# Cross attention in a four-layer perceiver: one sum over heads for four batches, the last key's share as a fifth slot, and the output product one round later

## The reference

```python
qh, kh, vh = heads(norm(x) @ wq.T + bq), heads(ctx @ wk.T + bk), heads(ctx @ wv.T + bv)
scores = einsum('bhqd,bhkd->bhqk', qh, kh) / sqrt(8) + mask * -1e9
av = einsum('bhqk,bhkd->bhqd', softmax(scores), vh)     # 257 keys
x = x + av.reshape(B, 32, 128) @ wo.T + bo
```

## Time and profile before

| | |
|---|---|
| time, median of 3 runs | 3692.14 us (3683.45 to 3694.7) |
| profiled execution | 3689.13 us, of which the span 3687.2 us |
| PE busy | 2674.5 us (73%) |
| DVE busy | 2416.8 us (66%) |
| ACT busy | 1807.5 us (49%) |
| POOL busy | 1662.8 us (45%) |
| rounds of the three stages touched | 827.9 to 1300.5, 1699.5 to 2173.7, 2770.2 to 3240.4 us of the span (first projection to last addition) |

### The profile page before, as it was taken

One profiled execution on the slowest core, in us unless ns is written; L12 is line 12 of the kernel. 1 busy time (PEld: TensorE's weight loads), 2 busy tenths in 40 slices (PEclk: granted clock), 3 DMA queues, 4 the chain that ended last, 5 costly groups with the idle time before them and its releaser, 6 DMA issues. The chain is left out here.

```text
span 3687.2 us, 98216 instructions
## 1 busy us (share of the span) xinstructions
PE 2674.5 (73%) x27184; PEld 2116.8 (57%) x27185; DVE 2416.8 (66%) x8780; ACT 1807.5 (49%) x5569; POOL 1662.8 (45%) x1768
## 2 busy tenths in 40 slices
PE   5962577739999979757999970367748999978562
PEld 3741466626777669645777740256636777747552
DVE  5965711148999947646999976551148999969615
ACT  2451033328888723325888865213327777734221
POOL 2620055517777700004777740015526777736162
PEclk9975588969999979878999985559979999979665
DMA  2003043421111100201333300214434544400122
GB/s 79 1 0 96 25 118 111 117 75 40 37 37 36 28 7 0 109 0 52 72 74 72 74 25 0 55 42 116 112 87 113 110 111 111 101 1 1 35 88 69
DMA packets 209738, 224.95 MB, mean 61 GB/s; under 512 B 29651, under 2 KB 177619, under 8 KB 208948
## 3 DMA queue, kind: packets, MB, share of 16 engines
q1 hardware_dynamic: 196948, 197.56, 20.5%
q0 software_dynamic: 12672, 25.98, 2.8%
HBM read 201.68 MB, written 21.76 MB: 61 GB/s over the span
## 5 line engine op out<-in xcount | busy, mean ns | idle before, releaser
L1765 ACT ACTIVATE sx<-sx,nm 128x257 f32<-128x257 f32 x1536 | 770.5, 505 | 264.2 <-DVE nm L1809 264.2
L1680 POOL TENSOR_TENSOR sx<-sx,rs 128x1028 f32<-128x1028 f32 x384 | 731.9, 1906 | 372.0 <-DVE rs L1815 372.0
L1809 DVE CUSTOM_DVE_ANT_0 sx<-bank,rows 128x257 f32<-128x257 f32 x1024 | 393.1, 422 | 53.7 <-PE bank L1755 35.5
L247 POOL TENSOR_TENSOR rstd<-var,nhalf 128x16 f32<-128x16 f32 x24 | 69.7, 2905 | 775.3 <-DVE var L264 775.3
L1443 ACT ACTIVATE hT<-bank,B 128x128 f32<-128x128 f32 x714 | 206.0, 368 | 432.2 <-PE bank L1411 260.8
L1469 DVE TENSOR_TENSOR yb<-bank,b2s 128x128 f32<-128x128 f32 x159 | 46.4, 292 | 429.6 <-remote 230.5
L1765 ACT ACTIVATION_READ_ACCUMULATOR sx<-sx,nm 128x1 f32 x1536 | 290.3, 189 | 0.0
L1424 PE MATMUL bank<-W,hT 128*128 x1428 | 236.2, 313 | 60.6 <-ACT hT L1443 44.1
L1755 PE MATMUL bank<-kT,qb 32*128 32x257 f32 x3072 | 275.7, 428 | 6.0 <-DVE nm L1809 6.0
L1744 PE MATMUL bank<-pt,vs 128*32 128x128 f32 x6144 | 247.5, 278 | 40.1 <-ACT pt L1774 34.7
L1826 DVE COPY pt<-bank 128x512 f32<-128x512 f32 x384 | 263.6, 687 | 3.3 <-PE bank L1700 2.9
(11 more groups left out here) (391 smaller groups left out, 5924.8 us busy)
## 6 DMA issues: line engine op xcount, KB each, us to landing
ct<-in_ctxT SPq DMA_DIRECT2D x384, 128.5 KB
W<-in_L_w SPq DMA_DIRECT2D x159, 256.0 KB
rows<-rows_x SPq DMA_DIRECT2D x256, 128.5 KB
keep<-rows_keep SPq DMA_DIRECT2D x128, 128.5 KB
yg<-copy_outs SPq DMA_DIRECT2D x40, 256.0 KB
token_rows<-XN SPq DMA_DIRECT2D x24, 256.0 KB, 2.3
W<-in_L_w SPq DMA_DIRECT2D x39, 128.0 KB
wu<-in_up_w SPq DMA_DIRECT2D x1, 4608.0 KB, 14.1
```

The source lines that it names most:

```text
L1680: pool.tensor_tensor(sx[:, j, :, 0:KEYS], sx[:, j, :, 0:KEYS], rs[:, j, :].unsqueeze(2).to_broadcast([P, 4, KEYS]), ALU.mult).then_inc(p_r ...
L1765: ins = act.activation(sx[:, j, h, 0:KEYS], sx[:, j, h, 0:KEYS], ACT.Exp, bias=nm[:, j, h:h + 1], scale=-1.0, accum_out=sm[:, j, h:h + 1])
L1809: dve.tensor_tensor_reduce(sx[:, j, h, 0:KEYS], B[h][:, 0:KEYS], add, -1.0, 3.0e38, ALU.add, ALU.min, nm[:, j, h:h + 1]).then_inc(s_summed ...
```

## The change

`a` becomes a ring of two tiles, each with 4 batches of 5 blocks of 32 positions. L1854 writes blocks 0 to 3 of its batch. In round 1 one product of the spread probabilities with the last values goes to block 4 of all four batches; it replaces the four additions to `oT`. The sum over heads of every round is gone; in round 2 one `tensor_reduce` sums the 5 blocks of all four batches into `oT` (640 elements per partition in, 128 out), after the copy of the values and before L1854 (L1858 in the changed kernel). The output product and the addition to `X` move from round 2 to round 3. `DEPTH` grows by one, so each stage has one written-out round more at its end. The arithmetic is the same but for the order of five additions.

```diff
-                a = sb2("a", [P, 2, P])
+                a = sb2("a", [P, 2, 4, 5, S])
...
-                DEPTH = 7
+                DEPTH = 8
...
-                            pe.wait_ge(*x_added((x - 7) // 4 if isinstance(x, int) else i * (U // 4) + (r_ - 7) // 4))
+                            pe.wait_ge(*x_added((x - 8) // 4 if isinstance(x, int) else i * (U // 4) + (r_ - 8) // 4))
...
-                        if r_ % 4 == 2 and ok(x - 10):
-                            pe.wait_ge(*pl_ready((x - 10) // 4 + 1 if isinstance(x, int) else i * (U // 4) + (r_ - 10) // 4 + 1))
+                        if r_ % 4 == 3 and ok(x - 11):
+                            pe.wait_ge(*o_ready((x - 11) // 4 + 1 if isinstance(x, int) else i * (U // 4) + (r_ - 11) // 4 + 1))
...
+                        if r_ % 4 == 3 and ok(x - 11):
+                            tl = (x - 11) // 4 if isinstance(x, int) else i * (U // 4) + (r_ - 11) // 4
+                            dve.wait_ge(*y_psum(tl + 1))
+                            xt_ = X[:, bass.ds(tl, 1), :]
+                            dve.tensor_tensor(xt_, xt_, B[7][:, P:2 * P].unsqueeze(1), ALU.add).then_inc(x_added.sem, 1)
                         if r_ % 4 == 2 and ok(x - 10):
-                            t = (x - 10) // 4 if isinstance(x, int) else i * (U // 4) + (r_ - 10) // 4
-                            dve.wait_ge(*y_psum(t + 1))
-                            xt_ = X[:, bass.ds(t, 1), :]
-                            dve.tensor_tensor(xt_, xt_, B[7][:, P:2 * P].unsqueeze(1), ALU.add).then_inc(x_added.sem, 1)
-                        b, q = x - 6, (r_ - 6) % 2
-                        if ok(b):
-                            dve.wait_ge(*a_ready(b + 1))
-                            dve.tensor_reduce(oT[:, ((r_ - 6) % 4) * S:((r_ - 6) % 4) * S + S],
-                                              a[:, q].rearrange("p (j s) -> p s j", j=4), AX.X, ALU.add)\
-                                .then_inc(o_ready.sem, 1)
-                        b, q = x - 5, (r_ - 5) % 2
+                            tl, tq = (x - 10) // 4 if isinstance(x, int) else i * (U // 4) + (r_ - 10) // 4, (r_ - 10) % 8 // 4
+                            dve.wait_ge(*a_ready(4 * (tl + 1)))
+                            dve.wait_ge(*pl_ready(tl + 1))
+                            dve.wait_ge(*y_psum(tl))
+                            dve.tensor_reduce(oT[:].rearrange("p (b s) -> p b s", b=4), a[:, tq].rearrange("p b j s -> p b s j"),
+                                              AX.X, ALU.add).then_inc(o_ready.sem, 1)
+                        b, q, tq = x - 5, (r_ - 5) % 4, (r_ - 5) % 8 // 4
                         if ok(b):
                             dve.wait_ge(*av_psum(b + 1))
-
-                            dve.scalar_tensor_tensor(out=a[:, q].rearrange("p (j s) -> p j s", j=4),
+                            if q == 0:
+                                dve.wait_ge(*o_ready((b // 4 if isinstance(b, int) else i * (U // 4) + (r_ - 5) // 4) - 1))
+
+                            dve.scalar_tensor_tensor(out=a[:, tq, q, 0:4, :],
...
                         if r_ % 4 == 1 and ok(x - 9):
...
                             dve.wait_ge(*pl_psum(tl + 1))
-                            dve.wait_ge(*o_ready(4 * (tl + 1)))
-                            for k in range(4):
-                                to = oT[:, k * S:(k + 1) * S]
-                                ins = dve.scalar_tensor_tensor(out=to, in0=B[7][:, k * S:(k + 1) * S], scalar=VL[:, bass.ds(tl * 4 + k, 1)],
-                                                               in1=to, op0=ALU.mult, op1=ALU.add)
-                            ins.then_inc(pl_ready.sem, 1)
+                            dve.tensor_tensor(a[:, tq, :, 4, :], B[7][:, 0:P].rearrange("p (b s) -> p b s", b=4),
+                                              VL[:, bass.ds(tl * 4, 4)].unsqueeze(2).to_broadcast([P, 4, S]), ALU.mult).then_inc(pl_ready.sem, 1)
```

More of the change, by code:

```diff
@@ L1611, in xattn @@
                 pl_psum, pl_ready = sig("pl_psum", TILES), sig("pl_ready", TILES)
-                av_psum, a_ready, o_ready = (sig(n, N) for n in ("av_psum", "a_ready", "o_ready"))
+                av_psum, a_ready = (sig(n, N) for n in ("av_psum", "a_ready"))
+                o_ready = sig("o_ready", TILES)
                 y_psum, x_added = sig("y_psum", TILES), sig("x_added", TILES)
@@ L1859, in stages @@
                         if r_ % 4 == 1 and ok(x - 9):
-                            tl = (x - 9) // 4 if isinstance(x, int) else i * (U // 4) + (r_ - 9) // 4
+                            tl, tq = (x - 9) // 4 if isinstance(x, int) else i * (U // 4) + (r_ - 9) // 4, (r_ - 9) % 8 // 4
                             dve.wait_ge(*pl_psum(tl + 1))
-                            dve.wait_ge(*o_ready(4 * (tl + 1)))
-                            for k in range(4):
-                                to = oT[:, k * S:(k + 1) * S]
-                                ins = dve.scalar_tensor_tensor(out=to, in0=B[7][:, k * S:(k + 1) * S], scalar=VL[:, bass.ds(tl * 4 + k, 1)],
-                                                               in1=to, op0=ALU.mult, op1=ALU.add)
-                            ins.then_inc(pl_ready.sem, 1)
+                            dve.tensor_tensor(a[:, tq, :, 4, :], B[7][:, 0:P].rearrange("p (b s) -> p b s", b=4),
+                                              VL[:, bass.ds(tl * 4, 4)].unsqueeze(2).to_broadcast([P, 4, S]), ALU.mult).then_inc(pl_ready.sem, 1)
                     run(dve, stages)
```

## The result

| | before | changed |
|---|---|---|
| median | 3693.42 us (4 runs) | 3723.26 us (3722.15 to 3725.74, 4 runs) |
| ratio to before | | 1.0085, 95% interval 1.0064 to 1.0107 |
| profiled execution | 3689.13 us, span 3687.2 | 3722.15 us, span 3720.3 |

A forecast was written before the change was run, and what follows sets the result against it. Within a stage it took PE and DVE as both nearly full, with ACT or DVE's order closing each round. Its terms, -38.4 + 62.4 + 6 + 1 = +31 us, gave 3722 us, with a range of 3686 to 3752.

The forecast's parts named there:

- What closes a round: In the attention stages: ACT closes rounds 0 and 3, DVE's order round 1 (0.50 late); round 2 has no DVE slack.
- The gone sums of rounds 0 and 3: Removing these DVE sums, 0.29 us each, gains 0 us, since ACT closes those rounds.
- Round 1: On DVE, one product replaces four additions: -0.40 us per tile, -38.4 us in all, bounds -31 to -43.
- Round 2, the new sum: On DVE, the 640-element sum takes 1.22 us, 1.14 in the order; round 2 grows by 0.65, +62.4 us in all.
- The extrapolation from L1847: Price of the new sum: L1847's 367 ns plus 512 elements at 1.66 ns, the rate of L1278, gives 1217 ns.
- It is not made up later: Round 2's growth of 0.65 us stays on the path: the next round's chain from first masked minimum to reciprocal keeps 3.06.
- PE's lag in round 3: Late PE transposes and the output product behind them delay round 3: +0.06 us per tile, +6 us; bounds -0.08 to +0.20.
- The sum: Total of all terms over the three stages: +31 us on the profiled execution of 3689.13 us.
- A contiguous price: Rival: the new sum takes 0.82 us despite its 128-byte steps; kernel faster by 18 us, 3672 to 3674; chance 0.12.
- the surplus once per instruction: Rival: L1847's extra 80 ns is paid once, so the sum takes 0.90 us; 3680 to 3697, chance 0.10.
- PE in DVE's place: Rival: PE starts transposes late after each long sum and doesn't catch up: +0.3 per tile, +29 us more, 3750; chance 0.08.
- Five times L1847: Rival: the new sum's surplus grows with the number of groups: 1.84 us, round 2 +1.27, +91 us, 3783; chance 0.04.

The follow-up runs named there:

- quarters: The changed kernel with the long sum cut into four, one batch a round, and the output product in the round 2 after: 3649.97 us against 3680.11, ratio 0.9928.
- doubled product: The changed kernel with the product of round 1 made twice, first into a spare tile nobody reads: ratio 1.0082 to the kernel before.
- interleaved blocks: The changed kernel with the five blocks interleaved, so the long sum reads contiguously and two writes go in steps of 20 bytes: ratio 0.9998 to the kernel before.
- sums of two and three blocks: The changed kernel with the long sum over only 2 or 3 of its 5 blocks: sums of 416 and 584 ns; with 2, ratio 0.989 to before.
- run with the sum last: The changed kernel with the long sum moved behind the masking of the value product (L1858) in round 2: ratio 1.0044 to the kernel before.

## Why the prediction was right

*What closes a round* held as far as sign and place go: ACT in rounds 0 and 3 (but for every second round 3, where the reciprocal came 0.12 after ACT already before the change), DVE in round 1, and in round 2 DVE without slack. The gone sums of rounds 0 and 3 brought nothing, as said: the quarters have a sum there again, and these rounds are as long as before the change. DVE's total fell while the time rose; with the quarters it is level with the changed kernel's (2399.7 us against 2396.4) and the time is 1.6% lower.

*Round 1* was taken at -0.40; between reciprocals it is -0.44 and -0.48, as the product hands over after 0.20 and not 0.25. The doubled product shows that this measure can flatter. In the first stage round 2 began its first minimum 0.30 and 0.24 after a late reciprocal before, and now 0.32 and 0.35 after one that is nearly on time, so 0.02 and 0.11 of the gain are paid there. In the other two stages it is at most 0.03.

*Round 2, the new sum* was taken at 1.22 us and 1.14 in the order; it is 1.252 and 1.16 (1012.96 to 1014.12). Round 2 grew by 0.71 and 0.80 where +0.65 was put. On average over the first stage's loop, 0.68 of it lies between the first minimum and the reciprocal, and the rest is what round 1 hands on. The price came out near for a reason that is only half right. That the layout makes the surplus is shown by the interleaved blocks (809 ns) against the rest. That each step of 128 bytes costs 0.6 ns more is refuted by the sums of two and three blocks, which come at the contiguous price. The extrapolation from L1847 held since its runs of four already carry the surplus. That was luck: the rate was taken from an addition (L1278), and nothing in the rows said that it would hold from four to five.

*"It is not made up later"* was the step that failed. Some 0.33 us of the round's delay is made up at once, as the first minimum of round 3 starts 0.09 after the reciprocal, not 0.41. ACT's idle time ahead of its first exponential of round 3 shows it: it went from 0.56 (at 1006.50 before) to 0.87 (at 1014.91), 0.31 more, where the prediction said 0.6. The 0.33 is lost again to *PE's lag in round 3*, which the prediction had as a term of its own with +0.06 a tile (the bounds -0.08 to +0.20). From the first minimum of round 3 to the next reciprocal it now takes 0.35 and 0.49 us longer (the two rounds 3 of a pass, averaged over the first stage's loop). Rounds 3 and 0 together grew by 0.12, 0.16 and 0.18 us a tile in the three stages. So the two errors nearly cancel, as the run with the sum last shows, where the lag is gone and rounds 3 are 0.4 shorter.

The prediction gave two reasons for the lag, bank 6 held until L1858 and the output product behind the late transposes. The second has the smaller part: with the product late and nothing else changed, the same stretch grew by 0.12 in one of the two rounds 3 and not at all in the other, and the time by a ratio of 1.0002.

*The sum*: +31 was predicted, and the three stages gave +30.9. That they agree so closely is luck. From round 16 to round 127 of each stage, 28 of its 32 tiles, the changed kernel took 11.4, 8.9 and 11.3 us more, together 31.5. The prediction's 0.31 a tile gives 26 there. For the other 12 tiles and the ends of the stages it had +5, and they gave -0.6, of which about -3 is the low clock at the end of the first stage before. The additions to `X` make the same point. They lie 14.3 us apart on average from the first to the last, where 14.45 was said, but 14.7 apart within the loop. The 14.15 and 14.05 from which the prediction started had the short last rounds in them; within the loop it was 14.3 in these two stages.

*The rivals.* A contiguous price is refuted by the 1252 ns, and so is the surplus once per instruction. PE in DVE's place is seen, but only as the lag within round 3; PE's busy share fell. Five times L1847 (1.84 us) did not come.

## What to carry to other kernels

Price a merged instruction by the round that it lands in, not by what it saves in sum: here the merged sum took 41 us less of DVE than its quarters and made the kernel 1.6% slower, since the small pieces lay in gaps of other rounds. Before placing a long instruction in an order, ask which buffer the instruction behind it holds, and who waits for that. And a delay between two marker instructions isn't yet a delay of the path: look whether the gap behind the second one has shrunk.

## What the hardware showed that was not expected

- Sums on DVE over runs in steps of 128 bytes: 416 and 584 ns for 128 runs of two and three, the contiguous price within 30 ns; 1036 and 1252 ns for runs of four and five, where contiguous reading gives 687 and 820. With steps of 132 bytes, runs of five took 1257 ns.
- Writes in steps of 20 bytes: 128 columns cost 446 ns instead of 349, and 396 instead of 281.
- Between DVE's reciprocal and the next minimum, which does not need its result but has register and wait instructions ahead of it, 0.35 us pass or more if the reciprocal had waited for ACT. It was 0.24 and 0.30 behind the four short additions, 0.15 behind the doubled product and 0.08 behind the long sum. Wherever the last wait lay behind the reciprocal or just ahead of it, the minimum began 0.15 to 0.17 after that wait (loops of the kernel before, the changed one, the late product and the doubled product).
